# DLRM tower with pairwise interactions on one core: gather pauses, transpose places and the first tail layer

## The reference

```
e = stack([tbl_0[ids[:, 0]], ..., tbl_39[ids[:, 39]]], axis=1)      # (2048, 40, 64)
p = e[:, rowidx]; q = e[:, colidx]                                  # 780 pairs
z = einsum('bie,fie,bif->bi', p, param, q)                          # (2048, 780)
h = concatenate([z, dense_ctx], axis=1)
h = maximum(h @ W_top1 + b_top1, 0)                                 # 512
h = maximum(h @ W_top2 + b_top2, 0)                                 # 256
y = h @ W_top3                                                      # (2048, 1)
```

## Time and profile before

| | us |
|---|---|
| median of 3 runs (1293.32 to 1294.88) | 1294.3 |
| the profiled execution | 1294.41 |
| its span in the trace | 1292.6 |
| PE busy | 1193.0 |
| DVE busy | 1062.8 |
| ACT busy | 937.1 |
| POOL busy | 606.2 |

### The profile page before, as it was taken

How to read it: one execution, slowest core, us unless ns; L and a number is a source line. 1 busy time by engine, 2 the same in 40 slices (tenths; PEclk the granted TensorE clock), 3 DMA queues, 4 the chain that set the end, 5 groups by cost and what they waited for, 6 DMA issues and landing times.

```text
span 1292.6 us, 21674 instructions
## 1 busy us (share of the span) xinstructions
PE 1193.0 (92%) x5664; PEld 424.0 (33%) x5664; DVE 1062.8 (82%) x932; ACT 937.1 (72%) x7305; POOL 606.2 (47%) x646
## 2 busy tenths in 40 slices
PE   1479987989999999999999999999999999999979
PEld 0123322333333333333333333333333333333323
DVE  0239898879998888799999888899999888899970
ACT  0027878689757886889967886789967887789861
POOL 6776555555555555555545555555555555200000
PEclk9869999989999999999999999999999999999989
DMA  4112222222222222222222222222222222111100
GB/s 136 41 41 72 61 68 60 61 53 75 59 69 65 57 65 60 60 68 60 69 69 69 60 61 67 61 59 69 67 70 67 62 59 61 51 48 50 50 2 0
DMA packets 50547, 77.66 MB, mean 60 GB/s; under 512 B 14004, under 2 KB 14260, under 8 KB 50296
## 3 DMA queue, kind: packets, MB, share of 16 engines
q1 hardware_dynamic: 29936, 55.26, 14.1%
q0 software_dynamic: 20480, 21.01, 8.4%
q10 hardware_dynamic: 8, 0.01, 0.0%
HBM read 76.22 MB, written 0.01 MB: 59 GB/s over the span
## 4 chain that ended last, share of the span: by engine, by line
PE 62%; DVE 3%; issue 2%; ACT 1%; DMA 0%; POOL 0%; DVEq 0%; ACTq 0%
PE ring L542 20%; PE ring L548 18%; PE z_ps L561 11%; PE aux L480 6%; PE aux L512 2%; PE ring L480 2%; PE aux L487 2%; DVE prod L470 1%; ACT act_prod L395 1%; DVE sums L440 1%; DVE dve_prod L470 1%; PE aux L494 1%; PE ring L487 1%; PE aux L501 0%; PE ring L543 0%
## 5 line engine op out<-in xcount | busy, mean ns | idle before, releaser
L395 ACT ACTIVATE act_prod<-act_prod 128x64 f32<-128x64 f32 x3584 | 856.5, 243 | 88.1 <-DVE act_prod L470 86.7
L395 ACT ACTIVATION_READ_ACCUMULATOR act_prod<-act_prod 128x1 f32 x3584 | 680.9, 190 | 0.0
L470 DVE TENSOR_TENSOR prod<-ring,emb 128x1024 f32<-128x1024 f32 x448 | 519.0, 1217 | 128.9 <-PE ring L543 127.9
L348 POOL DMA_INDIRECT stage<-tbl,idx x384 | 363.2, 946 | 313.4 <-issue 199.9
L542 PE MATMUL ring<-emb,raw 64*128 64x512 f32 x896 | 444.5, 623 | 12.0 <-issue 4.7
L543 PE MATMUL ring<-emb,raw 64*128 64x512 f32 x896 | 444.6, 624 | 0.0
L548 PE MATMUL ring<-raw,emb 64*128 64x512 f32 x704 | 371.4, 630 | 1.5
L549 PE MATMUL ring<-raw,emb 64*128 64x512 f32 x704 | 371.4, 631 | 0.0
L348 POOL DMA_INDIRECT kept<-tbl,idx x256 | 242.3, 946 | 191.1 <-issue 103.7
L470 DVE TENSOR_TENSOR act_prod<-ring,kept 128x1024 f32<-128x1024 f32 x224 | 263.3, 1217 | 40.6 <-PE ring L549 39.5
L542 PEld LDWEIGHTS ring<-emb,raw 64*128 64x128 f32 x896 | 159.0, 191 | 239.7 <-issue 145.1
(11 more groups left out here) (33 smaller groups left out, 204.4 us busy)
## 6 DMA issues: line engine op xcount, KB each, us to landing
raw<-param_b SPq DMA_DIRECT2D x200, 256.0 KB
stage<-tbl,idx POOLq DMA_INDIRECT x384
kept<-tbl,idx POOLq DMA_INDIRECT x256, 2.5
W<-W1g SPq DMA_DIRECT2D x1, 1792.0 KB, 8.4
W<-W2t SPq DMA_DIRECT2D x1, 512.0 KB, 10.1
idx<-ids_t SPq DMA_DIRECT2D x1, 240.0 KB, 3.8
z<-dense_t SPq DMA_DIRECT2D x4, 32.0 KB, 2.5
idx<-ids_t SPq DMA_DIRECT2D x1, 80.0 KB, 1.9
```

Of the source, the lines that this page charges most:

```text
L348: pool.indirect_dma_start(to[:, t, E * (f % 2) : E * (f % 2) + E], None, tables[f], bass.IndirectOffsetOnAxis(ap=idx[:, c, f, t : t + 1], ...
L395: op = act.activation(part, part, ACT.Copy, accum_out=sums[:, t, at : at + 1])
L470: dve.tensor_tensor(to, ring[:, n % RING, :, :], by, ALU.mult).then_inc(prod_done, 1)
```

## The change

Three edits. `HASTY` goes from 11 to 80, so that all 80 duos have the one pause behind the first gather, and none the two. The loop that fills `DUO_AT` moves transposes by up to 3 units where a `sum_batch` stands within the last four units or at the unit itself (`apart`), where a free place is near and the duo is not needed within four units; for this the table `SUM_AT` is made ahead of it. In the tail, the first-layer matmuls of the first three tiles stand ahead of the turn of the last sums and its waits.

```
-HASTY = 11
+HASTY = 80
...
+def apart(at):
+    return not any(at - 4 <= x <= at for x in SUM_AT)
...
         DUO_AT[_c, _d] = _at
-        AUX_AT.setdefault(_at, []).append(("duo", _c, _d))
+        if _at < NU * _c + FIRST[_d] - 4:
+            DUO_AT[_c, _d] = next((_at + u for u in (0, 1, -1, 2, -2, 3) if apart(_at + u)), _at)
+        AUX_AT.setdefault(DUO_AT[_c, _d], []).append(("duo", _c, _d))
...
             sum_batch(last, NF - 1)
+            pe.wait_ge(z_saved, FGROUPS * NCH - 1)
+            for m in range(H1 // P - 1):
+                layer1(ring[:, m // 2, m % 2, :], last, m, range(NG - 2))
             pe.wait_ge(aux_saved, len(AUX))
             turn_sums(last, SGROUPS - 1).then_inc(tail_ready, 1)
-            pe.wait_ge(z_saved, FGROUPS * NCH - 1)
-            for m in range(H1 // P):
-                layer1(ring[:, m // 2, m % 2, :], last, m, range(NG - 2))
+            m = H1 // P - 1
+            layer1(ring[:, m // 2, m % 2, :], last, m, range(NG - 2))
```

More of the change, by code:

```diff
@@ L105 @@
             FIRST.setdefault(_d, _u)
+SUM_AT = {}
+for _c in range(NCH):
+    for _b, (_kind, _x) in enumerate(BATCHES):
+        if _kind == "fields" and (_c, _x) != (NCH - 1, NF - 1):
+            _next = BATCHES[(_b + 1) % NB][0]
+            SUM_AT[NU * _c + BATCH * _b + (6 if _next == "samples" else 5)] = (_c, _x)
+def apart(at):
+    return not any(at - 4 <= x <= at for x in SUM_AT)
 AUX_AT = {}
@@ L128 @@
         AUX_AT[next((u for u in range(_at, _at + 12) if clear(u)), _at)] = [(_x, _c, _n)]
[L132 to L137, removed]
 REDUCE_AT = {}
```

## The result

| | us |
|---|---|
| before, median of 4 runs beside it (1293.32 to 1294.88) | 1294.07 |
| after, median of 4 runs (1250.10 to 1251.77) | 1250.86 |
| ratio, 95% interval | 0.9666 (0.9649 to 0.9683) |
| span of the profiled execution after (before 1292.6) | 1250.0 |
| forecast | 1259.0 (1253 to 1268) |

What follows compares the result with a forecast made beforehand. Gathers were taken to bound the kernel until about unit 230, then DVE's work with PE's absences. From 1294.4 us, 27 for the pause, 3.7 for moves and 4.7 for the tail gave 1259.0 us, range 1253 to 1268.

Steps and rivals of the forecast that it cites:

- Edit 1: One pause per duo from duo 11 on ends DVE's gather stops, mostly in the first chunk: -27 us, ends 23 and 29.
- scaled to the 247 us that remain that is 4.5 us: DVE idle time of 1.6 us in a later 88 us stretch, scaled and subtracted from 30.9, leaving 26.4 us.
- PE's own waits for gathers, 28.3 us, bound it from the other side: PE's 14 waits for gathers from 140.8 to 415 us, taken as a second bound on the pause's gain.
- Edit 2: 41 duos' transposes move by one to three units, sparing DVE stops in chunks 1 to 3: -3.7 us, between +2 and -5.
- the third (300 to 303) comes to stand two units ahead of the next sum, so I count half: Of three 0.42 us DVE stops per chunk behind layer pieces, this one counts half: 1.04 us a chunk, 3.1 in three.
- some 0.2 us a chunk: DVE idle time from transposes right ahead of or behind a sum, removed by the other moves: 0.6 us in all.
- the end of +2: Edit 2's slow end: the stall returns at the next sum, and ACT, copying in line, waits up to three units longer.
- Edit 3: Tail: first-layer matmuls fill PE's 2.99 us wait, and 1.7 us of low clock return: -4.7 us, ends -3.0 and -6.
- Gathers still bind: Rival, 1276 us: more gathers in flight land later, a duo takes 12.8 us and 17 of 27 us stay; chance 0.07.
- The moves bring nothing: Rival, 1266 us: the moves only shift idle time, and the tail's clock stays low; chance 0.11.
- POOL and DVE in each other's way: Rival: denser gathers stretch DVE's instructions; 41 ns a step eats 38 us, 60 ns gives 1315 us; chance 0.03.
- slower than before: The rival outcome over 1297 us, expected through denser gathers stretching DVE's instructions; chance 0.03.

Runs made afterwards that it cites:

- two short pauses: Changed kernel with pauses behind each duo's first and fifth gather, one gather staying in flight: 1263.95 us, 0.9764 in time; with transposes at old places 1271.25 us, 0.9812.
- one drained pause: Changed kernel with each duo's one pause ahead of its first gather, when nothing is in flight (`AHEAD = 0`): 1262.88 us, 0.9757 in time; 1.1633 on late chip 13.
- lag_two: Changed kernel with POOL waiting only for the duo two before, so hardly pausing until buffers run out: 1.3395 of the kernel before on chip 10, 1.3423 on chip 13.
- two drained: Two pauses per duo from duo 11, each until all gathers landed: changed kernel with `HASTY = 11`, 0.9915 on chip 10; before with moves alone, 0.9945 on chip 13.

## Why the prediction was right or wrong, point by point

**What bounds.** Right. DVE's work hardly changed (261.1 and 264.5 us in the two chunks) and the time went down by DVE's stops. Gathers bound units 50 to 231: 31.9 of the 43.2 us lie there.

**Edit 1.** Supply (forecast 10.75 to 11.65, measured 10.7 to 11.1 us a duo up to duo 18 and 11.3 in the mean up to duo 27), POOL's wait for free buffers and the end of PE's waits came as said. The size did not: 27 taken, 29 as the upper end, 31.9 measured. The first chunk was to take 312 to 317 us and took 309.5. Two steps of the term failed. First, "scaled to the 247 us that remain that is 4.5 us": this floor was subtracted as what the first chunk would keep. Counted over every pair of neighbouring DVE instructions with more than 0.06 us between them, units 51 to 232 kept 2.3 us in 8 stops (before 31.7 in 31); the waits view shows none up to 340 us. The 1.6 us of the earlier trace rows are the stops at units 410 and 415 (0.28 and 1.34 us), and their counterparts 200 units earlier, 210 and 215, did stay, with the same lengths. But they come once in a chunk, and scaling by time counted them nearly three times; what else stayed are six stops of 0.10 to 0.14 us. Second, a stop was priced at its idle time; each costs up to 0.09 us more. 29.4 us of idle time and 23 stops at some 0.1 make the 31.9. And "PE's own waits for gathers, 28.3 us, bound it from the other side" was no bound: what PE loses at a gather is more for DVE when the ring has to be filled again. How the 31.9 us divide between pause and moves is open, as the pause alone wasn't run on a chip in time; the stops that moved places took away in the gather-bound first chunk (units 68, 86, 171 and 180: 0.14, 0.88, 0.15 and 0.14 us between the kernels with two short pauses) came back elsewhere there.

**Edit 2.** Direction right, size wrong: 3.7 forecast, 6.5 measured in units 231 to 799. The step "the third (300 to 303) comes to stand two units ahead of the next sum, so I count half" failed; it went in full, in each chunk (units 300, 500, 700). The stops of 0.14 us, put at "some 0.2 us a chunk", were four or five (0.6 to 0.7 us) in the second and third chunk and two in the fourth, and each stop again cost its overlap. The second chunk was to be 4 us shorter and the third 1; they are 5.2 and 2.4 us shorter. The forecast end of -5 was passed; the end of +2 has its only trace where gathers bind.

**Edit 3.** Right: 4.7 forecast, 4.5 measured from the last product on, and the same 4.5 with the tail alone on chip 9. The 2.99 us went in full. The clock's part is 4.5 - 3.0 = 1.5, of 1.7. Where it comes from shows in the granted clock after (last column but two), for three stretches from the last sum on:

```profile
1210.00:1213.30 3.30, 3.27 (x16) 0.59 (x16) 3.30 (x3) 3.30 (x29) 0.00 (x0) 0.56 0.00 0
1213.30:1216.80 3.50, 3.50 (x12) 1.80 (x9) 0.06 (x1) 3.50 (x28) 0.00 (x0) 0.93 0.00 0
1216.80:1220.00 3.20, 3.20 (x9) 1.37 (x8) 0.00 (x0) 0.10 (x1) 0.00 (x0) 1.00 0.05 10
```

The clock was at its lower level of 1.2 GHz in nearly all of the last sum, behind an idle 2.26 us, as it was before; but since PE then goes on without a break it stays up from 1213.8 on, where before it fell a second time. The Trainium skill ("TensorE: Matmul & The Clock Gate", Part 1: The HAM clock gate) has the throttled state as the default that activity lifts; this trace agrees, with 0.56 behind the idle stretch and 1.00 once PE had gone on working. The first fall is not in every execution. With one drained pause, in time, the tail from the last product took 38.0 us; PE in it:

```profile
1222.64 1.92 PE L569 MATMUL z_ps<-prod,sel 128*32 128x512 f32 x16 [2.27 <-DVE prod L478]
```

The same sum takes 1.92 us in place of 3.36, at a full clock and behind the same idle time; 1.7 us of tail hang on that. Over the kept traces the new tail took 38.0 us in five and 39.6 to 39.7 in eight, the old one 44.2 in five, 44.7 and 45.6. So 4.5 us is the edit's gain between the commonest forms; one execution against another can show 4.5 to 7.6.

**The rivals.** Gathers still bind: out, the pauses were 1.0 to 1.5 us up to duo 18, and the longer ones behind it (2.75 us at duo 19) made no transpose wait. The moves bring nothing: out behind unit 231, twice. POOL and DVE in each other's way: as it was put, through longer products, it is out (1.22 us everywhere), in time and late. But the case of slower than before did come, with the whole change on chip 10 and with its pause alone on chips 9, 10 and 13, by a mechanism that the one trace of before doesn't show: POOL's unbroken gathers hold up the news of PE's work. The reason I gave for its low chance, that instructions are no longer while POOL issues, says nothing about signals.

**The sum.** 31.9 for 27, 6.5 for 3.7, 4.5 for 4.7, and 0.2 lost in the start: the first two terms make the 7.7 us by which the forecast missed the gain, and each of them passed its own outer end.

## What to carry to other kernels

Price a stop of the engine that bounds at its idle time plus the overlap that back-to-back instructions have, and look up the stops that will stay one by one, by their place in the chunk, instead of scaling a stretch from elsewhere by its time. A change of one engine's pacing is to be measured on several chips: here the change with the tighter pacing is 3.3% faster on one chip and 30% slower on another. Moves and tail with the old pauses are the safer version: 0.9915 on chip 10, and about 11 us, 0.991, in time, as a sum of stretches that wasn't run. Moving a buffer-bound step away from another by one to three places pays where the ring between the engines has had time to fill, and pays nothing while an input binds.

## What the runs showed of the hardware that was not expected

- On chips 9, 10 and 13 the end of PE's work reached DVE and ACT up to 54 us late while POOL issued indirect gathers with pauses of about 1 us, in the worst stretches one product each 11.20 us, and the same step without any pause (`lag_two`); where signals are in time, a waiting DVE starts 0.05 us behind the end of PE's unit (before, unit 151: 300.76 and 300.81 us). PE's ends are modelled, so PE's matmuls themselves may have been late, and the profiler ran each time. Signals of DVE to PE took 0.05 us in the median on both kinds, and after on chip 10 all but one of the 72 that PE waited for came within 0.15 us.
- The delay hangs on how much POOL pauses: ratios of 1.34 with none, 1.26 to 1.30 with one short pause, 1.16 with one drained, 0.99 with two drained, against a kernel that is itself late (168.0 us in place of 110.0 up to unit 50, and 29.3 us more behind unit 231). Where a long pause of POOL ended the delay, half of the late products began 1.04 to 1.10 us after its last gather with two drained pauses, and 1.70 to 1.80 us with one.
- The issue of gathers kept its step of 1.25 us (0.94 to 0.95 busy, 0.30 between) on both kinds of chip, and one duo its 10.7 us where no buffer was waited for.
- TensorE's clock in one and the same place, behind an idle 2.26 us, was 0.56 in the profile of after and 1.00 in that of the kernel with one drained pause, whose tail is the same, and 1.7 us of the tail hang on it.
